# Reordering the left-over gate/up rows of a four-group fp32 feed-forward kernel

## The reference

```
x = x + L0_ffn(W0[cond] mixing of x)          # mixing per batch, then a 1024x1024 product plus low-rank terms
x = x + L1_ffn(L1_cond(x))
L1_cond:  gate = x Wg^T + 0.5 (x Ag^T) Bg^T    # Ag, Bg, Au, Bu, Ad, Bd are chosen per batch (rank 16)
          up   = x Wu^T + 0.5 (x Au^T) Bu^T    # Wg, Wu: 2752 x 1024
          act  = silu(gate) * up
          down = act Wd^T + 0.5 (act Ad^T) Bd^T
L1_ffn:   down sign(W)^T + bias
```

## Time and profile before

| what | value |
|---|---|
| median of three runs | 2098.78 us (2098.72 to 2102.67) |
| profiled execution: its span, first to last instruction | 2096.8 us |
| between that span and the median | 2.0 us |
| PE busy | 2029.1 us, 97% of the span |
| DVE busy | 1475.6 us, 70% |
| ACT, POOL busy | 744.1 us (35%), 520.8 us (25%) |
| DMA | 107 GB/s mean over the span |

### The profile page before, as it was taken

How to read it: one execution, slowest core, us unless ns; L and a number is a source line. 1 busy time by engine, 2 the same in 40 slices (tenths; PEclk the granted TensorE clock), 3 DMA queues, 4 the chain that set the end, 5 groups by cost and what they waited for, 6 DMA issues and landing times.

```text
span 2096.8 us, 36423 instructions
## 1 busy us (share of the span) xinstructions
PE 2029.1 (97%) x9336; PEld 1682.9 (80%) x9336; DVE 1475.6 (70%) x2422; ACT 744.1 (35%) x1394; POOL 520.8 (25%) x900
## 2 busy tenths in 40 slices
PE   5999899999999999999999999999999999999998
PEld 4777788888887888888888788888888778888886
DVE  3566777777567777777665777777756777777774
ACT  2143333333243333333234333333323443333320
POOL 1232222221142222222123222222113222222200
PEclk8899999999999999999999999999999999999999
DMA  7648444444154655444143655545414564445401
GB/s 199 179 105 156 96 105 106 105 105 98 51 143 96 137 111 111 108 105 100 51 120 87 127 113 111 111 111 111 98 58 124 101 141 111 106 107 111 101 22 41
DMA packets 312832, 224.26 MB, mean 107 GB/s; under 512 B 167992, under 2 KB 302008, under 8 KB 312736
## 3 DMA queue, kind: packets, MB, share of 16 engines
q1 hardware_dynamic: 276256, 194.91, 40.2%
q0 software_dynamic: 35328, 24.03, 6.2%
q10 hardware_dynamic: 1152, 4.19, 0.5%
HBM read 210.18 MB, written 12.58 MB: 106 GB/s over the span
## 4 chain that ended last, share of the span: by engine, by line
PE 78%; issue 8%; POOLq 7%; DVE 3%; ACT 2%; POOL 1%; DMA 1%; DVEq 0%; SPq 0%; ACTq 0%
PE ps L1131 23%; PE ps L1133 22%; PE ps L1132 22%; POOLq L398 6%; PE ps L1294 6%; PE ps L1181 2%; PE ps L1182 2%; DVE ps L748 1%; ACT lora_b L514 1%; PE ps L1157 1%; POOL nat_b L443 1%; PE ps L1155 1%; ACT split L541 0%; DMA nat_b<-L_cond_B_up 0%; DVE acc L888 0%
## 5 line engine op out<-in xcount | busy, mean ns | idle before, releaser
L1131 PE MATMUL ps<-x,split 128*128 128x512 f32 x1440 | 567.2, 394 | 18.3 <-DVE split L734 12.1
L1133 PE MATMUL ps<-x,split 128*128 128x512 f32 x1440 | 563.8, 392 | 0.0
L1132 PE MATMUL ps<-x,split 128*128 128x512 f32 x1440 | 563.3, 391 | 0.0
L541 ACT ACTIVATE split<-ps 128x512 fp32r<-128x512 f32 x368 | 218.9, 600 | 485.6 <-DVE ps L748 473.0
L1131 PEld LDWEIGHTS ps<-x,split 128*128 128x128 f32 x1440 | 272.8, 189 | 74.3 <-issue 13.2
L1133 PEld LDWEIGHTS ps<-x,split 128*128 128x128 f32 x1440 | 272.1, 189 | 59.1
L1132 PEld LDWEIGHTS ps<-x,split 128*128 128x128 f32 x1440 | 272.3, 189 | 57.3
L450 POOL DMA_DIRECT2D nat_ad<-L_cond_A_down x224 | 138.4, 618 | 595.2 <-issue 591.2
L1131 PE MATMUL ps<-hidden 128*128 128x512 f32 (+1 forms) x704 | 275.1, 391 | 6.7 <-DVE acc L942 6.7
L1132 PE MATMUL ps<-hidden 128*128 128x512 f32 (+1 forms) x704 | 274.5, 390 | 0.0
L1133 PE MATMUL ps<-hidden 128*128 128x512 f32 (+1 forms) x704 | 274.3, 390 | 0.0
(11 more groups left out here) (106 smaller groups left out, 2701.7 us busy)
## 6 DMA issues: line engine op xcount, KB each, us to landing
nat<-L_cond_W_gate SPq DMA_DIRECT2D x336, 128.0 KB
nat<-L_cond_W_up SPq DMA_DIRECT2D x336, 128.0 KB
nat_down<-L_cond_W_down SPq DMA_DIRECT2D x112, 384.0 KB
nat<-effective_weight SPq DMA_DIRECT2D x32, 512.0 KB
nat_a<-L_ffn_weight SPq DMA_DIRECT2D x96, 128.0 KB, 2.8
nat<-x SPq DMA_DIRECT2D x16, 512.0 KB
nat_b<-L_cond_B_gate POOLq DMA_DIRECT2D x224, 24.0 KB, 2.1
nat_b<-L_cond_B_up POOLq DMA_DIRECT2D x224, 24.0 KB, 2.1
```

The lines of the kernel that those rows point to most:

```text
L541: act.activation(dst, src, func).then_inc(piece_hi, 1)
L1131: pe.matmul(dst, a[0], b[0], start=first, stop=False)
L1132: pe.matmul(dst, a[0], b[1], start=False, stop=False)
L1133: return pe.matmul(dst, a[1], b[0], start=False, stop=last)
```

## The change

PE multiplies G0's weights directly behind REM's weights, and REM's adapter product comes after that. REM moves from bank 1 to bank 2. `down_rest` moves from ahead of part 0 into it, between U0's weight product and U0's adapter product; for this, part 0 is written out ahead of the loop of parts. HEAD gets G0 ahead of DREM. DVE and ACT do G0 right behind `rank(0)`, and `rank(1)`, DREM and ADREM behind it; DVE does the nine copies of `down_rest`'s sums behind S6, S7 and G1. SP's and POOL's programs keep their order; the waits in them that count pieces follow HEAD.

```
-HEAD = (["B"]*3 + ["AG"]*2 + ["AU"]*2 + ["REM"]*2 + ["BREM"] + ["DREM"]*2 + ["ADREM"]
-        + ["G0"]*2 + ["U0"]*2 + ["S6"]*2 + ["S7"]*2 + ["G1"]*2)
+HEAD = (["B"]*3 + ["AG"]*2 + ["AU"]*2 + ["REM"]*2 + ["BREM"] + ["G0"]*2 + ["DREM"]*2
+        + ["ADREM"] + ["U0"]*2 + ["S6"]*2 + ["S7"]*2 + ["G1"]*2)

 ACT act_rest: ps[..., 1, :] -> ps[..., 2, :]
 ACT group:    rank(g, 0); + unit(G0); + rank(g, 1); DREM pieces; ADREM piece; - rank(g, 1); - unit(G0); unit(U0)

 DVE group:
                 rank(g, 0)
+                weight_unit(g, 0, "G0", NAT_FIRST[0], SPLIT_GU)
+                rank(g, 1)
                 down_rest(g)
                 a_down_rest(g)
-                rank(g, 1)
-                weight_unit(g, 0, "G0", NAT_FIRST[0], SPLIT_GU)
                 weight_unit(g, 0, "U0", NAT_FIRST[1], SPLIT_GU + 1)
                 act_rest(g)
-                for i in range(9):
-                    down_add(g, 0, i)
                 sign_unit(g, 0)
                 sign_unit(g, 1)
                 weight_unit(g, 0, "G1", NAT_FIRST[2], SPLIT_GU + 2)
+                for i in range(9):
+                    down_add(g, 0, i)

 PE gate_up_rest:
+                pe.wait_ge(rank_sum, 3 * g + 1)
-                of_x1(ps[:, 1, :], SPLIT_REM, False)
+                of_x1(ps[:, 2, :], SPLIT_REM, False)
+            def gate_up_rest_adapter(g):     # the two waits and the two adapter products, into bank 2

 PE part_gate_up(g, q, meanwhile=None):
                     gate_up_weight(g, q, k, name, q if k > 2 else q - 1)
+                    if k == 1 and meanwhile is not None:
+                        meanwhile(g)
                     gate_up_adapter(g, q, k)

 PE group:
                 gate_up_rest(g)
+                pe.wait_ge(rank_sum, 3 * g + 2)
                 gate_up_weight(g, 0, 0, "G0", 0)
-                down_rest(g)
-                with pe.Fori(0, NQ - 1) as q:
+                gate_up_rest_adapter(g)
+                part_gate_up(g, 0, down_rest)
+                gate_up_weight(g, 1, 0, "nextG0", 0)
+                down_part(g, 0, False)
+                with pe.Fori(1, NQ - 1) as q:
```

More of the change, by code:

```diff
@@ L57 @@
 assert NAT_UNITS % NAT_SLOTS == SPLIT_UNITS % SPLIT_SLOTS == PART_UNITS % NAT_SLOTS == 0
-HEAD = (["B"] * 3 + ["AG"] * 2 + ["AU"] * 2 + ["REM"] * 2 + ["BREM"] + ["DREM"] * 2 + ["ADREM"]
-        + ["G0"] * 2 + ["U0"] * 2 + ["S6"] * 2 + ["S7"] * 2 + ["G1"] * 2)
+HEAD = (["B"] * 3 + ["AG"] * 2 + ["AU"] * 2 + ["REM"] * 2 + ["BREM"] + ["G0"] * 2 + ["DREM"] * 2
+        + ["ADREM"] + ["U0"] * 2 + ["S6"] * 2 + ["S7"] * 2 + ["G1"] * 2)
 PART = (["U1"] * 2 + ["D0"] * 2 + ["G2"] * 2 + ["D1"] * 2 + ["U2"] * 2 + ["D2"] * 2 + ["AD"] + ["nextG0"] * 2
@@ L605, in act_rest @@
                 act.wait_ge(rest_psum, g + 1)
-                act.activation(gated[0:64, :], ps[0:64, 1, :], ACT.Silu).then_inc(gate_read, 1)
+                act.activation(gated[0:64, :], ps[0:64, 2, :], ACT.Silu).then_inc(gate_read, 1)
                 act.wait_ge(rank_lo, START + 3 * g + 2)
-                copy(act_f[0:64, :], ps[64:128, 1, :]).then_inc(rest_moved, 1)
+                copy(act_f[0:64, :], ps[64:128, 2, :]).then_inc(rest_moved, 1)
                 act.wait_ge(up_read, START + ACTS * g + 1)
@@ L686, in group @@
                 rank(g, 0)
+                unit(g, 0, "G0", SPLIT_GU)
+                rank(g, 1)
                 c = first_of("DREM")
@@ L692, in group @@
                 piece(g, 0, c, lora_ad[0:64, 0, 0, :], bank_of(c)[0:64, 0:P])
-                rank(g, 1)
-                unit(g, 0, "G0", SPLIT_GU)
                 unit(g, 0, "U0", SPLIT_GU + 1)
@@ L1206, in gate_up_rest @@
                 for t in range(2):
-                    mm = adapter_product(ps[:, 1, :], [lora_b_rem[:, kind, t, :] for kind in range(3)], t, t == 1)
+                    mm = adapter_product(ps[:, 2, :], [lora_b_rem[:, kind, t, :] for kind in range(3)], t, t == 1)
                 mm.then_inc(rest_psum, 1)
@@ L1237, in gate_up_adapter, with part_gate_up @@
                     .then_inc(up_psum if t else gate_psum, 1)
-            def part_gate_up(g, q):
+            def part_gate_up(g, q, meanwhile=None):
                 gate_up_adapter(g, q, 0)
```

## The result

The changed kernel takes 2107.66 us (median of 6 runs, 2104.01 to 2109.54); the kernel before took 2099.35 us beside it (median of 6). The ratio is 1.0029 [1.0018, 1.0041]: 0.3% slower. The forecast was 2094.6 us with a range of 2090.3 to 2099.5; the time lies outside it, on the other side of no change.

The account below looks back on a forecast made before the run. PE, busy 97% of the span, was taken as the bound, with holes mostly in group heads. Groups 0 to 3 at 0, -2.3, -2.3, +0.45 sum to -4.15, taking 2098.8 to 2094.6 us, range 2090.3 to 2099.5.

Parts of the forecast that it names:

- (a): Head: G0 early, REM's adapter later; both PE holes and the slow clock go, -6.6 us in group 1.
- (b): U0 next in the head: PE waits for U0's low part, +1.0 us.
- (c): down_rest behind U0's weights, copies behind G1: PE waits for the first copy, +1.1 us; last copy ends at 678.2.
- (d): Start of part 0: U1's load lands at 681.4, so DVE gains 2.3 us in groups 1 and 2, not 4.5.
- the prediction's own sign against (d): Start of part 0: (d) is wrong if DVE's wait for U1 is under 1 us.
- (e): POOL's loads: start +3.4 us, gain ceiling about 3.2 in groups 1 and 2; group 0 gains 0, group 3 loses 0.45.
- The prediction's sign against (e): (e) is wrong if group 0's restart moves over 1.5 us or group 1's nextB waits over 2.
- (f): Peeled part and list order: PE's extra code costs 0, at worst 6 us.
- Group 0 stayed where it was: Group 0: nextB stays at 209.76 and PE's restart at 216.62, gain 0.
- Slower: nextB: Rival, chance 0.06: in part 0, ADREM's wait and denser DMA traffic slow POOL's 24 loads beyond the 3.4 us counted.
- s = 3: Case of Slower: nextB with the 24 loads 3 us slower than counted: +3, +3.45, 0, 0 us, giving 2105.
- the rival of the falling clock: Rival, chance 0.07: clock falls in the new wait ahead of U1 in groups 1 and 2, +0.9 us twice, 2096.4.

Follow-up runs that it names:

- experiment 4: Changed kernel with down_rest's products over all 128 rows instead of 64 (output not the reference's): 2109.08 us, 1.0036 of the kernel before.
- experiments 9 and 10: Own buffer for ADREM's rows plus load_b_down at the end of POOL's group, in the changed kernel (2082.66 us) and in the kernel before (2087.1 us).
- experiment 6: Changed kernel with SP holding back the next part's down columns until nextB's loads have landed: 2092.48 us, 0.9965 of the kernel before.
- experiment 1: Changed kernel with an own buffer and semaphore for ADREM's rows, so POOL's load_ad need not wait: 2098.71 us, 0.9997 of the kernel before.
- experiment 3: Changed kernel with DREM and ADREM back ahead of G0 and the second rank step, all else kept: 2100.28 us, 1.0004 of the kernel before.
- experiments 9 and 11: Changed kernel with own ADREM buffer and load_b_down at the end of POOL's group (2082.66 us); the same with U1 loaded ahead of the sign tile (2079.51 us).

## Why the prediction was wrong

By its own steps:

- **(a) G0 early: right.** G0's pieces were to be turned at 652.65, `rank(1)` masked at 655.3, U0 turned at 661.85; they stand at 652.67, 655.27 and 661.83. Both holes and the slow starts behind them are gone in groups 0 to 2, the single hole in group 3.
- **(b) U0: right.** The hole was to be 1.0 us; by the distance of the starts it is 0.5 to 1.04.
- **(c) `down_rest`: right in the hole, not in the clock.** By the starts, PE waits 0.6 us in group 1 and up to 0.9 in the others ahead of its fourth tile (1.1 foreseen). That the product would then run at half clock was not foreseen. DVE's copies follow it 1.28 us apart, and DVE is free at 680.76 and not at 678.2. That this cost nothing is luck: U1 had not landed yet (experiment 4).
- **(d) U1's landing: right; what surrounds it: not.** 681.4 us forecast, 681.79 measured. But DVE was to wait 3 us for it and waits 1.02 (0.61, 1.58 and none in groups 0, 2 and 3), so that the prediction's own sign against (d), under 1 us, is just missed in group 1 and met in groups 0 and 3. PE was to wait 2 to 3 us ahead of U1 and 1.6 at nextG0; it waits not at all and 0.23. Where nextB doesn't interfere, groups 1 and 2 gain 2.7 and 2.9 us (experiments 9 and 10) against the 2.3 of (d).
- **(e) POOL: this step failed.** The prediction said that the last nextB load "goes from 704.04 to 707.4 and lands some 2.6 us after" and that "this queue allows 2.0". It was issued at 709.91 and landed after 4.9. Three terms were too small: POOL's start (663.25 forecast, 663.82), the 24 loads (44.2 us, as in the kernel before; 46.1) and the landing (2.6, what group 0 has before, 207.16 to 209.76; 4.9). The errors add up to 4.8 us: nextB was to be 2.0 us earlier than before and was 2.8 later. The last two have one cause, which experiment 6 shows: the 3.4 us that I did count pushed the loads into SP's burst, which itself came 2 us sooner. With that burst held back the 24 loads take 44.8 us, the last is issued 1.3 us sooner in the group and lands in 2.25. The prediction's sign against (e), nextB waited for in group 1 by over 2 us, was met with 4.81. The Trainium skill (DMA: Bandwidth & Descriptors, Queues, rings and completion order) says that each DMA engine takes turns between the queues at every packet. I would have read from it that a small DMA of POOL passes SP's large ones quickly; it gives no time for that, and the 4.9 us (changed kernel) and 6.1 (experiment 1) measured behind the burst in group 1, against 2.25 without it, do not bear my reading out. I had taken a load's cost as a constant, where it depends on what is on the queues when it is issued. The trace of the kernel before would have told: in group 3 its last load landed 5.6 us after its issue (1709.97 to the 1715.59 of the earlier trace rows), already inside a burst.
- **The clock behind the new hole was priced only for the wait ahead of U1.** It fell behind nextB's hole: eight slow starts in groups 0 to 2, six in group 3, 1.3 to 1.7 us each time (those of group 0 stood there before the change too). In group 1, nextB's 2.8 us less the 1.2 that DVE used to wait for PE at the first `down_add`, and 1.7 for the slow starts, make 3.3 us against the 2.95 measured.
- **(f) The peeled part: 0, as far as is known.** PE has no hole over 0.4 us between part 0 and part 1 in group 1 of the changed kernel, and the times of experiment 3 show no cost. No run has the peeled part alone.
- **Group 0 stayed where it was, as forecast.** Its nextB came at 209.69, forecast unchanged from 209.76.

The rival that came true is "Slower: nextB", with its place (POOL's loads in part 0) and its cause (ADREM's wait and the denser DMA traffic). It had a chance of 0.06. It gave 2105 for s = 3, but that it lies near the 2107.66 is luck: it had 3 us in group 0 and 3.45 in group 3 and nothing in groups 1 and 2, where the profile has nothing in group 0 and 2.65 to 2.95 in each of the others, and s was 4.8 us in group 1. The argument against it, that "the loads' number and place are unchanged", is where the chance went wrong. Their place in the list was unchanged, but not their place in time against SP's list. In the rival of the falling clock the Trainium skill (TensorE: Matmul & The Clock Gate, HAM oscillation) was cited for the clock's recovery being paid at each wait between bursts. The trace agrees for the new holes of 2.44 to 3.10 us, each of which was followed by 1.3 to 1.7 us of slow starts, at another gap than the one I tied it to; the holes of 1.73 and 2.17 us in experiment 1 paid nothing.

## What to carry to other kernels

A reordering moves two queues against each other, even if neither list changes. Before costing a late transfer at its usual landing time, look at what the other queue sends in those few microseconds, and take the landing from a row in which the two overlap. A wait for a shared staging buffer is worth nothing while the waiting engine comes late to it, and the whole chain behind it once the order changes. When two queues collide, holding back the large transfer that nobody needs yet (here one wait on SP, 13 to 15 us in the changed kernel) can be worth more than starting the small ones sooner. And a cost that is hidden by a late transfer (here the slow stretch in `down_rest`) is not gone: it came out, at some 3 us a group, as soon as the transfers were early.

## What the runs showed of the hardware

- **Small DMAs beside a burst.** POOL's nextB loads land 1.9 to 2.25 us after their issue when the DMA moves 12 to 25 GB/s (experiment 6). The six issued from 701.86 on in group 1 of the changed kernel took 4.3 to 6.1 us, with over 200 GB/s moving. The last load of a group took 3.8 us (changed kernel, group 3) to 6.1 (experiment 1, group 1) in a burst, and 2.7 where the burst ended just then (changed kernel, issued at 206.96 in group 0). The engine that issues is held as well: 3.96 us idle between two pairs at the burst's start where 1.85 is usual.
- **A 64-row product behind a short wait mostly lowers the clock.** In the changed kernel a wait of 0.45 us followed by 64-row matmuls ran at a granted clock of 0.50 (1.2 GHz). In the eight kernels that have this order with 64 rows, 27 of the 32 groups fell in `down_rest`, with waits of 0.41 to 0.81 us; five groups with waits just like these kept 1.00 (group 1 of experiments 9 and 11 among them), and nothing in the rows tells why. The kernel before issues the same 27 matmuls with no wait ahead and the clock stays at 1.00; with 128 rows and waits of 0.62 to 1.05 us (experiment 4) it stays at 1.00 in all four groups too.
- **Holes near the edge.** Waits of 1.73 us (715.96) and 2.17 (1716.16) in experiment 1 were followed by full clock, those of 2.30 us (experiment 3, 1726.72), 2.44 and more by slow starts. Of the hole's length alone these rows can't say more, since what PE did before it differs.
